# The fill of a linear attention: products without a reader, single modulation operations, statistics moved behind the running sum

## The reference, cut to what matters

```
mod = (silu(c) @ wmod).reshape(2, 6, 1, 128)             # per layer; sa, ca, ga, sb, cb, gb
ga = (2 * (ga >= 0) - 1) * maximum(abs(ga), 0.25)        # the same for gb
h = layernorm(x) * (1 + ca) + sa
q, v = silu(h @ Wq), h @ Wv
log_f = log_sigmoid(h @ Wk + delta); k = -expm1(log_f)
S = S * exp(log_f_t) + k_t v_t ;  o_t = q_t S            # a recurrence over 2048 steps, 2 heads of 64
o = rmsnorm(o * sigmoid(h @ G1 @ G2)) * norm_w
x = x + ga * (o @ Wo)
```

## Time and profile before

| | |
|---|---|
| three runs | 1144.08, 1151.99, 1155.32 us; median 1151.99 |
| profiled execution | 1151.95 us, span 1150.2 us |
| busy share of the span | PE 92%, PEld 63%, DVE 77%, ACT 74%, POOL 59% |
| mean granted TensorE clock | 0.965 of full speed |
| linear attention's 32 running sums (L421) | first at 18.6 us, last at 181.9 us |

### The profile page before, as it was taken

How to read it: one execution, slowest core, us unless ns; L and a number is a source line. 1 busy time by engine, 2 the same in 40 slices (tenths; PEclk the granted TensorE clock), 3 DMA queues, 4 the chain that set the end, 5 groups by cost and what they waited for, 6 DMA issues and landing times. The chain is left out here.

```text
span 1150.2 us, 33841 instructions
## 1 busy us (share of the span) xinstructions
PE 1057.9 (92%) x11683; PEld 727.5 (63%) x11683; DVE 890.7 (77%) x2963; ACT 849.7 (74%) x2674; POOL 679.9 (59%) x1082
## 2 busy tenths in 40 slices
PE   5899998799999999899799999999899899999996
PEld 3676765367777776566477777776566488853442
DVE  4789996688888888665688888888685645289998
ACT  5578885499888888533688988988445776478886
POOL 3988995599888888410688888888232500012222
PEclk9579998799999999999999999999999999999998
DMA  7000000011312211141112122121101352100000
GB/s 244 2 2 8 15 3 1 19 43 42 72 43 55 55 46 35 46 139 31 40 38 57 39 48 48 39 48 38 32 2 39 81 128 84 30 8 17 17 17 18
DMA packets 66498, 50.86 MB, mean 44 GB/s; under 512 B 42262, under 2 KB 53442, under 8 KB 66050
## 3 DMA queue, kind: packets, MB, share of 16 engines
q1 hardware_dynamic: 66339, 48.84, 16.7%
HBM read 21.41 MB, written 2.38 MB: 21 GB/s over the span
## 5 line engine op out<-in xcount | busy, mean ns | idle before, releaser
L1222 PE MATMUL psum<-wa_wqkv,wa_hT 128*128 128x512 f32 x384 | 191.5, 608 | 2.5 <-DVE wa_tmp L1086 1.3
L1178 ACT ACTIVATE wa_p<-psum,wa_nb 128x128 f32<-128x128 f32 x512 | 184.1, 399 | 2.0 <-DVE wa_nb L1102 1.7
L1102 DVE CUSTOM_DVE_ANT_0 psum<-psum,wa_bias 128x128 f32<-128x128 f32 x512 | 132.8, 322 | 50.1 <-PE psum L1251 50.1
L1067 POOL TENSOR_TENSOR wa_p<-wa_p,wa_rrs 128x512 f32<-128x512 f32 x128 | 133.5, 1043 | 41.4 <-DVE wa_rrs L1111 41.4
L1767 POOL TENSOR_TENSOR ex_total<-ex_total,mod 128x128 f32<-128x128 f32 x32 | 15.5, 485 | 204.2 <-DVE ex_total L1895 204.2
L1038 POOL TENSOR_TENSOR wa_qr<-wa_qr,wa_tmp 128x512 f32<-128x512 f32 x64 | 81.8, 1279 | 79.4 <-DVE wa_tmp L1086 79.4
L1178 ACT ACTIVATION_READ_ACCUMULATOR wa_p<-psum,wa_nb 128x1 f32 x512 | 122.3, 239 | 0.0
L1942 ACT ACTIVATE cv_z_ex_yw<-psum,ex_w 128x128 f32<-128x128 f32 x384 | 107.0, 401 | 19.8 <-DVE ex_w L1871 7.3
L2013 PE MATMUL psum<-ex_wc,ex_hT 128*128 128x512 f32 x256 | 117.7, 603 | 3.4 <-DVE cv_z_ex_yw L1878 2.1
L1188 ACT ACTIVATE wa_pT<-psum 128x512 f32<-128x512 f32 x128 | 76.4, 597 | 37.1 <-PE psum L1231 37.1
L1231 PE MATMUL psum<-ident,wa_p 128*128 128x128 f32 x512 | 79.3, 277 | 9.6 <-ACT wa_kT L1171 2.9
(11 more groups left out here) (262 smaller groups left out, 3015.3 us busy)
## 6 DMA issues: line engine op xcount, KB each, us to landing
wa_vm<-wa_v SPq DMA_DIRECT2D x127, 128.0 KB, 2.3
cv_toep<-cv_zpad SPq DMA_DIRECT2D x32, 136.0 KB, 2.6
cv_toep<-cv_zpad SPq DMA_DIRECT2D x16, 264.0 KB, 4.0
wa_tabs<-in_rotations_dram SPq DMA_DIRECT2D x2, 2048.0 KB, 8.0
wa_rows<-y_rows SPq DMA_DIRECT2D x31, 128.0 KB
wa_rows<-y_rows SPq DMA_DIRECT2D x31, 127.0 KB
x_rows<-in_L_attn_x_dram SPq DMA_DIRECT2D x4, 512.0 KB, 5.6
out_dram<-x_rows SPq DMA_DIRECT2D x32, 64.0 KB, 1.5
```

Source lines behind the costliest of these rows:

```text
L1067: nc.gpsimd.tensor_tensor(p, p, cols_bc(rrs[:, t % 2, r, :], P), ALU.mult)\
L1102: m = nc.vector.tensor_tensor_reduce(out=s, in0=s, in1=edges, scale=-1.0, scalar=MAX_FLOAT, op0=ALU.add, op1=ALU.min, accum_out=nb[:, t % ...
L1178: e = nc.scalar.activation(pr[:, t % 2, r, h, :], sim_bank[r][:, P * h:P * h + P], ACT.Exp, bias=nb[:, t % 2, r, h:h + 1], scale=-1.0, acc ...
L1222: nc.tensor.matmul(bank, hT[:, t % 3, :], wqkv[:, INNER * k:INNER * k + INNER], start=True, stop=True).then_inc(done.sem, 1)
```

## The change

A new function issues n products of the identity with a broadcast of the identity, 512 columns wide, into a PSUM bank; nothing reads the result. Five are issued: one in step 2 behind the value product, one at the head of step 3, two in step 3 behind the transpose, one at the head of step 4. The one in step 2 first waits for `REST`; the others stand behind waits that were there. GpSimd's rows are cut into six pieces of one operation, in steps 1 to 6 for layer 0 and 7 to 12 for layer 1; the gains come last, so the output weights wait for one operation fewer. On VectorE `next_statistics` moves from before the scaled queries to behind the running sum, still ahead of the query product.

```diff
--- before.py
+++ after.py
@@ -178,6 +178,12 @@
                 f(self.first + s - lag)
 
 
+def idle_products(c, bank, n):
+    for _ in range(n):
+        c.nc.tensor.matmul(bank[:, 0:BANK].rearrange("p (a b) -> p a b", b=P), c.ident[:, :],
+                           rows_bc(c.ident[:, :], BANK // P), start=True, stop=True)
+
+
 def interleaved(phases, timetable):
     for phase, s in timetable:
         phases[phase].step(s)
@@ -200,7 +206,7 @@
     G1T, GATE = 5, 6
     ROW_BANKS = ((4, 5), (6, 7)) * B
     MOD_COLS, WOG = [0], [0]
-    SIGNS, ROWS_DONE = (2 + GH, 8 + GH), (7 + GH, 13 + GH)
+    SIGNS, ROWS_DONE = (2 + GH, 8 + GH), (6 + GH, 13 + GH)
     MAX_STEP, MAX_SIG_LOG = 20.0, 41.0
     with ExitStack() as own:
         sb = c.sb(own)
@@ -335,23 +341,25 @@
             if piece == 0:
                 gp.wait_ge(a_set, ROW_COPIES[k])
                 nc.gpsimd.tensor_scalar(sign[...], mags, 0.0, 2.0, ALU.is_ge, ALU.mult).then_inc(g_set, 1)
+            if piece == 1:
                 gp.wait_ge(g_set, SIGNS[k])
                 nc.gpsimd.tensor_scalar(sign[...], sign[...], -1.0, None, ALU.add).then_inc(g_set, 1)
-            if piece == 1:
-                nc.gpsimd.tensor_scalar(gains, gains, 1.0, None, ALU.add).then_inc(g_set, 1)
+            if piece == 2:
                 gp.wait_ge(g_set, SIGNS[k] + 1)
                 nc.gpsimd.tensor_tensor(mags, mags, sign[...], ALU.mult).then_inc(g_set, 1)
-            if piece == 2:
+            if piece == 3:
+                gp.wait_ge(g_set, SIGNS[k] + 2)
+                nc.gpsimd.tensor_scalar(mags, mags, 0.25, None, ALU.max).then_inc(g_set, 1)
+            if piece == 4:
                 gp.wait_ge(g_set, SIGNS[k] + 3)
-                nc.gpsimd.tensor_scalar(mags, mags, 0.25, None, ALU.max).then_inc(g_set, 1)
-            if piece == 3:
-                gp.wait_ge(g_set, SIGNS[k] + 4)
                 nc.gpsimd.tensor_tensor(mags, mags, sign[...], ALU.mult).then_inc(g_set, 1)
+            if piece == 5:
+                nc.gpsimd.tensor_scalar(gains, gains, 1.0, None, ALU.add).then_inc(g_set, 1)
 
         def early(s):
             def f():
-                if s < 10:
-                    modulation_rows(s // 6, (s - 2) % 4)
+                if s < 13:
+                    modulation_rows((s - 1) // 6, (s - 1) % 6)
                 else:
                     gp.wait_ge(g_set, ROWS_DONE[1])
             return f
@@ -370,7 +378,7 @@
                 nc.gpsimd.memset(heads[hd(h), h:h + 1], 1.0 / GD).then_inc(g_set, 1)
 
         return Phase([(keys, 1), (modulate, 14), (distances, 1)], 0, TILES, begin=begin,
-                     between={**{s: early(s) for s in range(2, 11)}, 16: lambda: given.gpsimd(gp)})
+                     between={**{s: early(s) for s in range(1, 14)}, 16: lambda: given.gpsimd(gp)})
 
     def vector(dve):
 
@@ -533,8 +541,8 @@
             return f
 
         between = {s: early(s) for s in range(3, 9)}
-        return Phase([(y_statistics, 10), (base_level, 4), (clip, 1), (next_statistics, 1), (y_shift, 11), (scaled, 3), (residual, 9),
-                      (running_sum, 1), (update, 4), (gated, 4), (query, 1), (keep_levels, 3)], 0, TILES,
+        return Phase([(y_statistics, 10), (base_level, 4), (clip, 1), (y_shift, 11), (scaled, 3), (residual, 9),
+                      (running_sum, 1), (next_statistics, 1), (update, 4), (gated, 4), (query, 1), (keep_levels, 3)], 0, TILES,
                      between=between, begin=begin)
 
     def scalar(act):
@@ -697,6 +705,15 @@
             take("turn", a_h, t)
             nc.tensor.transpose(turn[:, 0:P], rows[:, t % 3, :], c.ident[:, :]).then_inc(p_h.sem, 1)
 
+        def after_turn(t):
+            if t == 3:
+                idle_products(c, bk[4], 2)
+
+        def after_values(t):
+            if t == 2:
+                pe.wait_ge(a_set, REST)
+                idle_products(c, bk[4], 1)
+
         def project(t):
             if t == 0:
                 pe.wait_ge(a_set, GATE)
@@ -786,14 +803,17 @@
 
         def before_scores():
             pe.wait_ge(a_set, REST)
+            idle_products(c, bk[4], 1)
 
         def before_output():
             pe.wait_ge(a_set, ROW_COPIES[1])
+            idle_products(c, out, 1)
 
         def before_products():
             pe.wait_ge(v_set, WOG[0])
 
-        return Phase([(turn_h, 0), (output, 4), (scores, 3), (values, 1), (project, 0), (mean_squares, 5),
+        return Phase([(turn_h, 0), (after_turn, 0), (output, 4), (scores, 3), (values, 1), (after_values, 0),
+                      (project, 0), (mean_squares, 5),
                       (o_project, 8)], 0, TILES, longer=values, more=2,
                      between={1: early(1), 2: early(2), 3: before_scores, 4: before_output, 8: before_products}, begin=begin)
```

## The result

The changed kernel takes 1147.46 us (median of 20 runs, 1142.93 to 1154.22), the kernel before 1151.10 (20 runs, 1144.08 to 1156.57). The ratio is 0.996, 95% interval 0.9942 to 0.9979: the medians lie 3.6 us apart, the interval excludes no change, and the gain is smaller than the 1% named in the prediction. The forecast was 1143 us, a gain of 9; the range of 1137 to 1155 holds the result, but it also holds the kernel before. The lowest of the 20 runs differ by only 1.2 us (1144.08 and 1142.93): much of the gain is that long times are rarer.

The account below looks back on a forecast made before the run. The prediction took TensorE's lower clock from 25 to 70 us as the bound, GpSimd close behind. 10.4 less 0.5 gave 9.9 us if the clock held, 8.4 if recovered; it took 9: 1143 us, range 1137 to 1155.

Parts of the forecast that it names:

- What bounds the fill: From 25 to 70 us TensorE at 1.2 GHz (granted clock 0.51) bounds the fill, GpSimd close behind, 42.95 of 45 busy.
- Statistics: Statistics behind the running sum: tile 2's projection 1.1 us later, step 3's scaled queries about 28.3 instead of 29.93; an exchange.
- GpSimd: One modulation operation per step, steps of 5.1 or 6.1 us; about 4 us behind the running sum by step 11.
- The rival that made it the bound: Clock holds but GpSimd's lag reaches the decays at step 8; gain 6 to 7 us, 1145; chance 0.08.
- The output weights: no cost: Output weights wait for one GpSimd operation fewer, done a step before them as now, so they cost nothing.
- The products: Five products in TensorE's waits of steps 2 to 4: free at full speed, or 3.6 us in all at half.
- What the clock gives at the end of the fill: Tile 3's to tile 9's projection in 30.5 us against 39.9; 9.9 us gained if clock held, 8.4 if recovered.
- the 0.5 given back for GpSimd: Loss of 0.5 us because GpSimd's lag by step 11 slightly exceeds the slack before a tile's decays are wanted.
- Does it fall again: Rival: clock falls again in steps 5 to 7, giving back 3 to 5 us: 1147; chance 0.16.
- after the first table step the wait is about 0.8 us: Ground against the clock falling again: that wait is no more than steady steps have.
- The rival "slower": Clock falls at 26 us and stays down; products cost 2.7 us in step 3, 0.9 in step 4: 1155.6; chance 0.12.
- the first sentence of the sum: A microsecond gained at the fill's end counts fully at the kernel's end, as nothing behind has an absolute time.

Follow-up runs that it names:

- cut kernels: Four kernels ended after linear attention; medians: before 218.70 us, changed 210.89, changed without products 215.19, before with only the five products 214.97.
- pieces back: Changed kernel with GpSimd's modulation rows as before, two operations in the first two steps of each layer; 1150.14 us, ratio 0.9972 to the kernel before.
- statistics back: Changed kernel with VectorE's statistics again between the clip and the scaled queries; 1149.60 us, ratio 0.9969 to the kernel before.
- shifted: Changed kernel with 40 empty instructions ahead of TensorE's first wait; 1148.84 us, ratio 0.9978 to the kernel before.
- more products: Changed kernel with five more wide products, one heading each of steps 5 to 8, one behind step 6's transpose; 1144.55 us, ratio 0.9936.
- all three: Changed kernel plus five products in steps 5 to 8, six at linear attention's end, and statistics behind the query product; 1143.34 us, ratio 0.9926.

## Why the prediction was right or wrong, point by point

**What bounds the fill** was right. The clock was the bound: with it, the steps from the projection of tile 3 to that of tile 9, but for step 6, take 4.5 to 5.2 us each for 6.7 to 7.2 (5.4 in the last, in which the clock came back). Without it (products of two columns) the ratio is 0.9996. That the clock is the whole gain isn't shown: the kernel without products had it low for 30.7 us and has 0.996, with an interval (0.9936 to 0.9985) that overlaps the other's.

**Statistics.** Projection of tile 2 forecast at 26.6, measured 26.39; scaled queries of step 3 at about 28.3, measured 27.94; the query there at 32.1, measured 31.69. The earlier trace rows had 29.93 for the scaled queries. The exchange was read rightly. What it was worth was not: the text called it an exchange and gave it nothing. The two moves together gained 1.4 to 3.5 us in the cut kernels without any product, where the low stretch ended at 56.5 us and not at 71.5. With products of two columns it ended at 70.3 in spite of both moves, so whether the moves end it earlier, or executions differ, stays open.

**GpSimd.** It lags as forecast: keys of tile 8 start at 64.74, 3 us behind their running sum at 61.79. The rival that made it the bound had these keys at 65.6 and the projection of tile 9 near 66.5; that projection is at 63.69, so the lag didn't reach the path. "The output weights: no cost" holds. With the products alone they waited 0.44 us for GpSimd, part of a longer wait behind which the clock fell; with the pieces back they didn't wait, but GpSimd held TensorE up at 58.70 us, by way of ScalarE (2.53 us).

**The products.** Forecast free at full speed but for up to 1.1 us under the cover of the query. Measured: the pair behind the transpose ends at 29.99 (30.4 forecast), the scores at 31.15 (31.6), and the projection at 32.11 still waits 0.48 us for VectorE. Right.

**What the clock gives at the end of the fill.** Forecast 9 to 9.9 us, projection of tile 9 at 63 to 65; measured 9.7 and 63.69. Right in sum, with errors that offset: the six steps took 31.6 us, not 30.5 (7.1 for 6.3 in step 6, in which the clock fell), and the projection of tile 3 came at 32.11, not 32.5; the 0.5 given back for GpSimd wasn't seen up to there.

**Does it fall again.** The place was named (step 6, before the output) and the chance was too small: 0.16 for something that every trace of a full kernel with the five wide products shows: the clock falls in step 6 and comes back within 4 us in the changed kernel and with the statistics back, falls twice with the pieces back, and stays down 20 us with the products alone and in the shifted kernel. With it the median is probably a mixture, and the likeliest single case isn't the median. That the rival's figure, 1147, is nearly the median is in part luck: it priced this fall alone, and part of the loss lies in the convolution. The text's grounds against it, "after the first table step the wait is about 0.8 us", looked past step 6 itself. The rival "slower" is answered by the four traces in which the clock was low at the first product: it was back within 3.5 us.

The Trainium skill, "TensorE: Matmul & The Clock Gate", section "The HAM clock gate", says that the point of transition differs between runs, by half a microsecond either way. Between kernels with the same fill the traces differ by much more: 3.4 against 20.4 us at half clock behind waits of 1.14 and 1.15, in the changed kernel and in the one with 40 empty instructions ahead.

**The step that failed** is the first sentence of the sum: "I take a microsecond gained at the end of the fill as a microsecond gained at the end". It was the term of 9 us that was mis-sized: measured 3.6 between the medians, 6.4 between the profiled executions. Of the 9.7 gained in the profiled execution, none was lost on the way to the convolution and 3.9 in it. "Nothing behind it is tied to an absolute time" was true and beside the point: the change adds instructions to TensorE's program, and that isn't nothing for work 900 us later. The list of waits of ten kernels shows it (the last column runs from the convolution's first record to its last):

| kernel | TensorE instructions added ahead | "issue" in the convolution, us | convolution, us |
|---|---|---|---|
| before | none | 0.4 | 76.4 |
| without products | none | 0.4 | 78.0 |
| changed kernel | five products | 2.2 | 80.3 |
| products alone | five products | 2.8 | 79.4 |
| statistics back | five products | 2.9 | 83.7 |
| pieces back | five products | 2.3 | 79.0 |
| two columns | five small products | 2.6 | 79.5 |
| shifted | five products, 40 empty instructions | 2.9 | 79.6 |
| more products | ten products | 2.1 | 79.7 |
| all three | 16 products | 1.5 | 77.5 |

Five products are 20 records of instructions (products and weight loads): the changed kernel has 33861 and the kernel before 33841, and without the products it is 33841 again. The row of the changed kernel:

```profile
PE psum L2289 <- issue: 2.2, 4, 1.2
```

What goes with the holes is the instructions' being there, not what they compute and not the clock in the fill: products of two columns have the holes, and so has a fill at full clock. Two things in the kept traces point to how TensorE's instructions are brought to it. First, the place. In the six kernels with five products the two long holes stand before the same records of the convolution, the 1280th and the 1532nd of 2048; with five products more, 10 records earlier; with eleven more, the one that is left stands 22 earlier, half of the 20 and 44 records of instructions added. Second, the time. The profile has a queue of its own for instructions (q8, 88 pieces of 16384 bytes in each full kernel), and each of these 15 holes, 0.3 to 1.5 us long, ends 1.25 to 1.52 us behind the landing of such a piece. So the holes are bound to places in the program and very likely are waits for instructions. Why the pieces come late only with products added stays open, and the 40 empty instructions, which left the holes at the same records, don't fit. In the profiled execution the 3.9 us are the three holes of the second batch (1.8), 0.4 in the products beside them (16.0 us for 15.59), and 1.6 us of a clock that fell behind the longest hole. That fall isn't part of the rule: with the products alone and with the pieces back a hole as long (1.2 us) has none behind it, and in the four kernels with five products and no fall in the convolution it takes 2.6 to 3.2 us more than in the kernel before. The durations of the last column also hold falls of the clock (most in the kernel with the statistics back) and small waits for other engines, so they don't follow the holes one to one; the kernel without products has no holes but the common one and still 1.6 us more than before, 1.0 of it between the two batches, where the clock fell from 947.3 to 950.7 us, and the rest unexplained.

**The rest**, from 6.4 to 3.6 us, is that the profiled execution lies 1.9 us under the median of its kernel's 20 runs and that of the kernel before 0.9 over its own. In full kernels the products' own gain can't be seen: without them the ratio is 0.996 too. At the end of linear attention they earn between nothing and 3.7 us alone, and 3.1 to 4.3 on top of the moves, by the readings of the cut kernels; in the convolution they pay 2.6 us or more. The kernel with ten products, in which the fall of step 6 is gone, has a median 2.9 us lower than the changed kernel's (on another chip) and less than half its spread, though the intervals of the two ratios overlap (0.9909 to 0.9964 and 0.9942 to 0.9979).

## What to carry to other kernels

Products that nobody reads, standing in the waits of the fill, held TensorE's clock here, or brought it back within 3.5 us, when they were 512 columns wide, and did neither with two. In one wait of 1.1 us left open the clock fell again; with products there the spread shrank from 11 to 4 us and the median was another 3 us lower, though the intervals overlap. Check what else a quicker stretch makes late (here GpSimd's results, which had been early enough), since the clock just won can fall again in the wait that this makes. And count an added instruction as a change to all code behind it: a gain at one place is not a gain at the end until the later phases are compared block by block.

## What the runs showed of the hardware that wasn't expected

- With 20 to 64 records of instructions added to TensorE's program 900 us ahead, the convolution had 1.5 to 2.9 us of "issue" waits in eight kernels of eight; the two without had 0.4. Their places in the program moved with the number of products added, and each long one ended 1.25 to 1.52 us behind the landing of a piece of instructions.
- The busy share didn't tell the clock: 41.68 of 45 us busy at 0.51 with products of two columns, 37.82 of 45 at 0.96 with 512.
- One and the same wait (1.14 or 1.15 us) went with 3.4 us at half clock in two traces and with 20.4 in another.
- Wide products met at the low clock in four traces were followed by full clock within 3.5 us; without wide products it took 30.7 or 44.4 us in five.
